# Graph and feed-forward kernel: early weight loads, a bias and a table copy moved into the first convolution, node tables in seven pieces

## What is computed

```python
def gcn_conv(x, W, b, src, dst, num_nodes):
    h = x @ W
    loop = jnp.arange(num_nodes, dtype=src.dtype)
    s = jnp.concatenate([src, loop]); d = jnp.concatenate([dst, loop])
    deg = segment_sum(ones, d)
    dinv = rsqrt(deg)
    msg = h[s] * (dinv[s] * dinv[d])[:, None]
    return segment_sum(msg, d) + b

h = gcn_conv(layernorm(x), W1, b1, src, dst, 6250)      # 256 -> 128
h = relu(h)
x = x + gcn_conv(h, W2, b2, src, dst, 6250)             # 128 -> 256
```

## Time and profile before

| | before |
|---|---|
| median of 3 runs | 4726.0 us (4722.5 to 4734.35) |
| the profiled execution's own time | 4731.23 us |
| its span | 4729.4 us |
| PE, DVE, ACT, POOL busy | 59%, 50%, 16%, 56% |
| mean granted TensorE clock | 0.743 of full speed |

### The profile page before, as it was taken

How to read it: one execution, slowest core, us unless ns; L and a number is a source line. 1 busy time by engine, 2 the same in 40 slices (tenths; PEclk the granted TensorE clock), 3 DMA queues, 4 the chain that set the end, 5 groups by cost and what they waited for, 6 DMA issues and landing times. The chain is left out here.

```text
span 4729.4 us, 52933 instructions
## 1 busy us (share of the span) xinstructions
PE 2773.6 (59%) x12432; PEld 2169.6 (46%) x12432; DVE 2355.0 (50%) x5207; ACT 743.6 (16%) x1703; POOL 2645.2 (56%) x2784
## 2 busy tenths in 40 slices
PE   1333344433233333444548989968887877844998
PEld 0333333333233333333437744446666666632665
DVE  5533333333433333333645344448777777864344
ACT  0200000000000000000324422223333333312222
POOL 2777777777477777777440042147777777741000
PEclk9755666556655556666669999978888888875999
DMA  5122222222222222222323355444444444430000
GB/s 112 44 59 53 53 53 53 53 53 53 62 53 53 53 53 53 53 53 51 107 98 111 104 187 190 181 142 138 138 139 138 138 138 134 138 98 23 16 16 23
DMA packets 200796, 410.20 MB, mean 87 GB/s; under 512 B 51652, under 2 KB 125012, under 8 KB 193589
## 3 DMA queue, kind: packets, MB, share of 16 engines
q0 software_dynamic: 102144, 246.72, 19.3%
q1 hardware_dynamic: 98356, 160.05, 10.5%
HBM read 305.82 MB, written 104.44 MB: 87 GB/s over the span
## 5 line engine op out<-in xcount | busy, mean ns | idle before, releaser
L657 POOL DMA_INDIRECT ring<-t_gcn,idx x1568 | 1479.5, 944 | 545.0 <-issue 476.9
L683 PE MATMUL psum<-ring,big 128*128 x3328 | 770.7, 421 | 1281.7 <-SPq L666 1261.3
L683 PEld LDWEIGHTS psum<-ring,big 128*128 128x128 f32 x3328 | 707.0, 320 | 1345.3 <-issue 1344.5
L700 DVE TENSOR_TENSOR big<-big,psum 128x128 f32 x1664 | 480.6, 289 | 1257.3 <-PE psum L683 1065.0
L1509 POOL DMA_INDIRECT xs_ring<-t_msg,idx x832 | 801.5, 963 | 381.4 <-issue 252.5
L1637 PE MATMUL psum<-xs_ring,a_hot 128*128 128x264 f32 x1456 | 410.1, 442 | 0.0
L1637 PEld LDWEIGHTS psum<-xs_ring,a_hot 128*128 128x128 f32 x1456 | 332.8, 229 | 75.3
L1393 PE MATMUL psum<-big,a_xnt 128*128 128x512 f32 x784 | 354.4, 595 | 0.5 <-ACT a_xnt L1365 0.5
L1298 POOL DMA_INDIRECT a_back<-t_y,m_addr x98 | 97.7, 997 | 439.2 <-POOLq L1102 280.8
L831 ACT ACTIVATE m_xa<-big,dinv 128x128 f32<-128x128 f32 x49 | 19.4, 400 | 2028.3 <-PEq L643 2028.3
L412 DVE TENSOR_TENSOR big<-dloc,psum 128x1024 f32<-128x1024 f32 x210 | 254.8, 1214 | 26.3 <-PEq L709 13.1
(11 more groups left out here) (378 smaller groups left out, 3927.1 us busy)
## 6 DMA issues: line engine op xcount, KB each, us to landing
t_msg<-a_rows SPq DMA_DIRECT2D x49, 1056.0 KB, 3.9
a_near<-t_near SPq DMA_DIRECT2D x52, 512.0 KB, 4.1
ring<-t_gcn,idx POOLq DMA_INDIRECT x1568, 2.5
m_xin<-t_tok SPq DMA_DIRECT2D x105, 128.0 KB, 2.1
t_y<-m_yb SPq DMA_DIRECT2D x105, 128.0 KB, 2.1
xs_ring<-t_msg,idx POOLq DMA_INDIRECT x832, 2.8
xs_ring<-in_x SPq DMA_DIRECT2D x7, 896.0 KB, 11.1
t_gcn<-big SPq DMA_DIRECT2D x2, 3136.0 KB, 12.5
```

Of the source, the lines that this page charges most:

```text
L657: g.indirect_dma_start(out=ring[:, q % 4 * 8 + j, :], out_offset=None, in_=t_gcn[conv], in_offset=bass.IndirectOffsetOnAxis(ap=idx1[:, q * ...
L683: t.matmul(ps[j % 4][:, 0:HID], hot[q % 2][:, j, :], ring[:, at[j], :], start=True, stop=True).then_inc(s_used.sem, 1)
L700: v.tensor_tensor(a_n, a_n, ps[j % 4][:, 0:HID], ALU.add).then_inc(s_added.sem, 1)
```

## The change

Five things are edited. (1) `w1`, `b1`, `b2` and `dst_firsts` (now `firsts_i`) get buffers that live through both convolutions, and SP loads them and W2 in the first stage, behind the seven pieces of `x`; it waits for all five before it stores `same`. (2) The store of `near` is issued right behind that of `same`, and SP waits for both; the eight copies to `t_same8` leave the first stage. (3) In the first convolution ACT issues these eight copies at its start and waits for them at the end. (4) POOL's 49 additions of `b2` are removed; in the first convolution DVE adds `b2` to all of `xs` in one instruction, in its third turn (`q == 2`), between the selection matrices and the eight additions of that turn. (5) The scalings ahead of both tables go group by group, and SP stores each group (seven tiles) when it is ready; between the convolutions the three passes are interleaved over the groups.

```diff
                     for g in range(NG):
                         sp.dma_start(xs[:, g * GT:(g + 1) * GT, :], xr[...]).then_inc(s_ld[1].sem, 16)
+                    sp.dma_start(firsts_i[:], dst_firsts).then_inc(s_in.sem, 16)
+                    sp.dma_start(w1[:], g_w1.rearrange("(k p) f -> p k f", p=P)).then_inc(s_in.sem, 16)
+                    sp.dma_start(gw2[:], g_w2).then_inc(s_in.sem, 16)
+                    sp.dma_start(b1[:], g_b1.to_broadcast([P, HID])).then_inc(s_in.sem, 16)
+                    sp.dma_start(b2[:], g_b2.to_broadcast([P, D])).then_inc(s_in.sem, 16)
                     sp.wait_ge(s_ld[1].sem, s_ld[1].base + 16 * NG)
+                    sp.wait_ge(s_in.sem, s_in.base + 80)
                     sp.wait_ge(s_d.sem, s_d.base + SCH)
                     sp.dma_start(t_same..., same[:]).then_inc(s_same.sem, 16)
-                    sp.wait_ge(s_same.sem, s_same.base + 16)
                     sp.dma_start(t_near..., near[:]).then_inc(s_same.sem, 16)
-                    for h in range(HEADS):
-                        sp.dma_start(t_same8[:, :, h, :], t_same.rearrange("(b j) e -> b j e", j=SBS)).then_inc(s_same.sem, 16)
+                    sp.wait_ge(s_same.sem, s_same.base + 32)
...
-                    @b.sync
-                    def _(sp):
-                        sp.dma_start(first_i[:], dst_firsts).then_inc(s_ld[0].sem, 16)
...
-                        sp.wait_ge(s_in.sem, s_in.base + 64)
...
-                        g.wait_ge(s_in.sem, s_in.base + 64)
-                        with g.Fori(0, NG) as i:
-                            for j in range(GT):
-                                n = i * GT + j
-                                g.wait_ge(s_dve.sem, s_dve.base + n + 1)
-                                g.nop(nofuse=True)
-                                g.tensor_tensor(xs[:, n, :], xs[:, n, :], b2[:], ALU.add)
...
-                        v.wait_ge(s_ld[0].sem, s_ld[0].base + 16)
-                        v.tensor_copy(first[:], first_i[:]).then_inc(s_stage.sem, 1)
+                        v.tensor_copy(first[:], firsts_i[:]).then_inc(s_stage.sem, 1)
...
-                        v.tensor_tensor(acc[:], acc[:], dinv[:]..., ALU.mult).then_inc(c.sem, c.up())
-                        v.wait_ge(c.sem, c.value())
+                        for g in range(NG):
+                            n = slice(g * GT, (g + 1) * GT)
+                            v.tensor_tensor(acc[:, n, :], acc[:, n, :], dinv[:, n]..., ALU.mult).then_inc(s_a.sem, 1)
...
+                        for g in range(NG):
+                            n = slice(g * GT, (g + 1) * GT)
+                            sp.wait_ge(s_a.sem, s_a.base + g + 1)
+                            sp.dma_start(rows_of[:, n, :], acc[:, n, :]).then_inc(s_out.sem, 16)
+                        sp.wait_ge(s_out.sem, s_out.base + 16 * NG)
...
+                    if conv == 0:
+                        @b.scalar
+                        def _(a):
+                            for h in range(HEADS):
+                                a.dma_start(t_same8[:, :, h, :], t_same.rearrange("(b j) e -> b j e", j=SBS)).then_inc(s_same.sem, 16)
+                            a.wait_ge(s_same.sem, s_same.base + 16 * HEADS)
...
                             build_hot(v, hot[1 - q % 2][:], q * 8 + 8, ps[7][:, 0:P]).then_inc(s_hot.sem, 1)
+                            if conv == 0 and q == 2:
+                                v.tensor_tensor(xs[:], xs[:], b2[:].unsqueeze(1).to_broadcast([P, NT, D]), ALU.add).then_inc(s_dve.sem, 1)
+                                v.wait_ge(s_dve.sem, s_dve.base + 1)
...
+                            for g in range(NG + 2):
+                                for stage in range(3):
+                                    p = g - stage
+                                    if not 0 <= p < NG:
+                                        continue
+                                    n = slice(p * GT, (p + 1) * GT)
+                                    dv = dinv[:, n].unsqueeze(2).to_broadcast(wide)
+                                    if stage == 0:
+                                        v.tensor_tensor(acc[:, n, :], acc[:, n, :], dv, ALU.mult).then_inc(s_a.sem, 1)
+                                    if stage == 1:
+                                        v.wait_ge(s_a.sem, s_a.base + p + 1)
+                                        v.tensor_tensor(acc[:, n, :], acc[:, n, :], b1[:]..., ALU.add).then_inc(s_b.sem, 1)
+                                    if stage == 2:
+                                        v.wait_ge(s_b.sem, s_b.base + p + 1)
+                                        v.scalar_tensor_tensor(acc[:, n, :], acc[:, n, :], 0.0, dv, ALU.max, ALU.mult).then_inc(s_d.sem, 1)
```

More of the change, by code:

```diff
@@ L203, in gnn_ffn_kernel @@
         freed = sb("freed", [1, HALVES], I32, gcn_rows)
+        w1 = sb("w1", [P, KD, HID], F32, gcn_rows)
+        b1 = sb("b1", [P, HID], F32, gcn_rows)
+        b2 = sb("b2", [P, D], F32, gcn_rows)
+        firsts_i = sb("firsts_i", [P, -(-ETP // P)], I32, gcn_rows)
         def row_statistics(v):
@@ L235, in _ @@
                 def _(sp):
-                    sp.dma_start(first_i[:], dst_first).then_inc(s_in.sem, 16)
+                    sp.dma_start(first_i[:], dst_first).then_inc(s_ld[2].sem, 16)
                     sp.dma_start(idx1[:], src_e).then_inc(s_ld[0].sem, 16)
@@ L274, in _ @@
                     v.memset(same[:, :, P:LINK], 1.0).then_inc(s_c.sem, 1)
-                    v.wait_ge(s_in.sem, s_in.base + 16)
+                    v.wait_ge(s_ld[2].sem, s_ld[2].base + 16)
                     v.tensor_scalar(first_i[:], first_i[:], 7, None, ALU.arith_shift_right).then_inc(c.sem, c.up())
@@ L366, in gnn_ffn_kernel @@
             s_pool.after(4)
-            s_in.after(16)
+            s_in.after(80)
+            s_ld[2].after(16)
             s_ld[0].after(16)
@@ L374, in gnn_ffn_kernel @@
             s_act.after(SCH)
-            s_same.after(16 * (2 + HEADS))
+            s_same.after(32)
             for k in range(SCH):
@@ L418, in gnn_ffn_kernel @@
             hot = [big[:, NT * HID + k * 8 * P:NT * HID + (k + 1) * 8 * P].rearrange("p (s e) -> p s e", e=P) for k in range(2)]
-            w1 = sb("w1", [P, KD, HID], F32, ph)
-            b1 = sb("b1", [P, HID], F32, ph)
             xn = [sb(f"xn{k}", [P, D], F32, ph) for k in range(4)]
@@ L433, in gnn_ffn_kernel @@
                 deg = sb("deg", [P, NT], F32, dg)
-                first_i = sb("first_c", [P, FT], I32, dg)
                 first = sb("first", [P, FT], F32, dg)
@@ L445, in gnn_ffn_kernel @@
                 prev = sb("prev", [P, 2, P], F32, dg)
-                b2 = sb("b2", [P, D], F32, dg)
                 LATE = NT - GT
@@ L561, in _ @@
                         t.wait_ge(s_d.sem, s_d.base + 2 * NG)
-                        t.wait_ge(s_in.sem, s_in.base + 64)
                         with t.Fori(0, NG) as i:
@@ L600, in _ @@
                                     a.copy(acc[:, i * GT + j - 2, :], ps[4 + (j - 2) % 4][:, 0:HID]).then_inc(s_e.sem, 1)
-                s_in.after(64)
-                s_ld[0].after(16)
                 s_pool.after(2)
@@ L627, in _ @@
                         v.wait_ge(c.sem, c.value())
-                        v.tensor_tensor(acc[:], acc[:], dinv[:].unsqueeze(2).to_broadcast([P, NT, HID]), ALU.mult).then_inc(c.sem, c.up())
-                        v.wait_ge(c.sem, c.value())
+                        for g in range(NG):
+                            n = slice(g * GT, (g + 1) * GT)
+                            v.tensor_tensor(acc[:, n, :], acc[:, n, :], dinv[:, n].unsqueeze(2).to_broadcast([P, GT, HID]), ALU.mult).then_inc(s_a.sem, 1)
                     @b.sync
                     def _(sp):
-                        sp.wait_ge(s_dve.sem, s_dve.base + 3)
-                        sp.dma_start(t_gcn[0].rearrange("(n p) f -> p n f", p=P), acc[:]).then_inc(s_out.sem, 16)
-                        sp.wait_ge(s_out.sem, s_out.base + 16)
+                        rows_of = t_gcn[0].rearrange("(n p) f -> p n f", p=P)
+                        for g in range(NG):
[3 more added lines that the diff above has]
+                        sp.wait_ge(s_out.sem, s_out.base + 16 * NG)
                 s_act.after(1)
-                s_dve.after(3)
-                s_out.after(16)
+                s_dve.after(2)
+                s_a.after(NG)
+                s_out.after(16 * NG)
             for conv in range(2):
@@ L700, in _ @@
                                 v.tensor_tensor(a_n, a_n, ps[j % 4][:, 0:HID], ALU.add).then_inc(s_added.sem, 1)
+                if conv == 0:
+                    s_same.after(16 * HEADS)
+                    s_dve.after(1)
                 s_used.after(STEPS + 16)
@@ L711, in _ @@
                         def _(v):
[L712 to L718, removed]
@@ L719, in _ @@
-                            v.scalar_tensor_tensor(acc[:], acc[:], 0.0, dv, ALU.max, ALU.mult).then_inc(c.sem, c.up())
-                            v.wait_ge(c.sem, c.value())
```

(16 more changed lines are left out.)

## The result

The changed kernel takes 4673.45 us, median of four runs (4671.83 to 4678.53), the kernel before 4725.7 us. The ratio is 0.9888, 95% interval 0.9871 to 0.9906: 52 us or 1.1% faster. The forecast was 4675 us.

A forecast was written before the change was run, and what follows sets the result against it. The prediction took POOL's gather queue to bound both convolutions. Its terms, -20.7 - 8.1 - 22.9 - 5.4 - 6.4 + 12.5 = -51.0 us, set against the median of 4726.0 us, gave 4675 us, range 4657 to 4690.

The forecast's parts named there:

- The start of the degree stage and its end: Degree stage: nodes no longer late behind the queued copies, -8.1 us; without POOL's additions the next block starts sooner, -22.9 us.
- The first stage: First stage: both stores land by 69.5 us, the next block starts at 70.1 instead of 90.76 us, -20.7 us.
- The first table: Scaling and store before the first convolution: seven pieces start the 12.5 us stream (some 2 fixed) earlier, -5.4 us.
- The second table: Between the convolutions: 21 pieces of 1.04 us, then a last store of 4.4 us, 26.3 instead of 32.7 us, -6.4 us.
- The copies: First convolution: ACT's eight copies beside the first gathers cost 0, up to +3 us if late landings and the addition meet.
- rival B: First convolution: the copies slow POOL's issue itself, giving 4709 us (chance 0.04) or 4743 us (chance 0.02).
- The bias: First convolution, third turn: DVE's 13.2 us addition with two on-chip inputs holds a POOL gather, +12.5 us (0 to +13.3).
- Rival A: First convolution: DVE's long addition doesn't hold POOL, so the sum is -63.5 and the time 4662 us; chance 0.17.
- Rival C: Stage ends: barriers stay where they are, held by another engine or POOL's drain; 4697 us if half of 43.6 stays; chance 0.05.

The follow-up runs named there:

- bias-on-POOL runs: Changed kernel with only the move of the bias undone, POOL adding b2 tile by tile in the degree stage: 4686.51 us on an ordinary chip; also run on the slow chip.

## Why the prediction was right

- **The start of the degree stage and its end** (-8.1, -22.9) came out at -8.1 and -22.8. The 4.3 us between POOL's last addition and the barrier went with POOL's loop, as taken. That the 8.1 us were the queue and not the load is now shown.
- **The first stage** was 1.0 us better than taken: `near` landed with `same`, within 68.5 us, not at 69.5. DVE ends at 68.5 us too, so this stage has no more to give by SP alone.
- **The first table**: -5.4, by a stream that starts one piece in. The seven stores were issued over 8.13 us, the last landed 13.8 us behind the start of the first product (within 14, as forecast), and the gathers began 15.9 us behind L604. The "some 2 us fixed" of the step stood on no row: by a store of 448 KB landing in 3.0 us when nothing is beside it and one of 3136 KB in 12.5 us, an estimate is 1.4.
- **The second table**: mis-sized, -6.4 taken and -7.9 measured. Half of the difference is the last store's landing, 4.4 us by the row of `same` and 3.6 as measured (the seven stores landed in 3.0 us in the median; the 3.3 of the page is of both tables). The other half is the pieces, which follow each other at 1.00 us, not 1.04: 21 of them end 21.1 us behind the first start, not 21.9. DVE's first two and last two pieces, and the stores of this stage alone:

```profile
1179.74 2.09 DVE L724 TENSOR_TENSOR big<-big,dinv 128x896 f32<-128x896 f32 x2 [0.32 <-PEq L633]
...
1198.79 2.08 DVE L730 SCALAR_TENSOR_TENSOR big<-big,dinv 128x896 f32<-128x896 f32 x2
...
t_gcn<-big SPq DMA_DIRECT2D x7, 448.0 KB, 3.0
```

- **The copies**: 0, shown by moving them, though they delay the first landings by 8 us. POOL's issue didn't change beside them, so rival B falls.
- **The bias**: +12.5 taken, 12.6 of hold measured. The step rested on a transfer of 1.35 us that had met additions of 0.42 us, on one of 4.71 us beside a memset of 3.47 us, and on scaling these to 13.2 us. Rival A (no hold, 4662 us) is what the version with the bias in PSUM does: 4658.67 us.
- **Not in the sum**: 3.2 us inside the degree stage. POOL's additions had held DVE: the last seven normalisations took 4.9 us from first to last instead of 2.8, L527 6.28 us instead of 5.75, L538 and L540 0.62 instead of 0.2. Single instructions (shortest, median and longest in ns; L521 and L477 before the change, L509 behind it):

```profile
L521 DVE TENSOR_SCALAR xn<-xs_ring,mean,rstd x7: 414/818/907, 174.9 to 179.1; 128x256 f32 x7
...
L509 DVE TENSOR_SCALAR xn<-xs_ring,mean,rstd x7: 405/411/414, 145.5 to 147.8; 128x256 f32 x7
...
L477 POOL TENSOR_TENSOR xs_ring<-xs_ring,b x49: 711/712/6229, 175.9 to 215.3; 128x256 f32 x49
```

  The normalisations beside POOL's additions took twice as long. The last row shows the other direction: one of POOL's additions took 6.23 us, beside L527 of 6.28 us, a DVE instruction with two inputs in on-chip memory. So the trace of before held a much longer case of this hold than the 0.42 us that the prediction scaled up. It used the mechanism in one direction and didn't look for it in the other. The bias-on-POOL runs agree: L527's counterpart took 6.28 us again, twice.
- **How near the forecast came** is in part luck. With these 3.2 us, the second table and the first stage the terms measured add up to 56.7 us, 5.7 more than the 51.0 of the sum, while the medians differ by 52.2 (on the last chip by 53.7). A remainder of 3 to 4.5 us, which no run explains, brings the measured time back to the forecast.
- Rival C (barriers stay) falls: L604 stands 0.5 us behind DVE's last instruction.

## What to carry to other kernels

Where POOL's gathers are the bound, a DVE instruction with two inputs in on-chip memory (13.22 us here), or at double pace (6.69 us), can hold their queue until it ends. Put one input of a two-input instruction into PSUM before moving work there, and if that can't be, cut it small. Look for a POOL transfer that is longer than its neighbours, and for the DVE instruction that it ended with: a hold of 0.4 us on a short one tells what a long one will cost. A load that seems slow at the start of a stage may only stand behind transfers that nobody waits for.

## What the runs showed that was not expected

- Additions on POOL, one behind the other, made one normalisation of DVE last 29.92 us instead of 0.41; it ended only when POOL waited on a semaphore.
- A gather that had started 0.5 us before a double-pace DVE instruction was held as well, until that ended (7.31 us), while one that had started 0.77 us before the two-input addition stayed at 0.94 us (215.33 and 216.10 us). Rows 7 had a first sign of it: the transfer of 4.71 us had started 0.28 us before its memset. At which points of its work a gather can be held is open.
- One of three chips took 5882 us for the kernel before, 24% more, with PE and DVE standing at times for no reason that the profile names; single instructions and transfers took as long as elsewhere (L527's counterpart 5.75 us, a gather 0.943, the store of a whole table 12.5). A comparison of totals across chips would have been worthless, and a bound had moved: POOL waited for slots there.
